# Expansion stage of a three-layer graph network: 0/1 matrices of four groups in one comparison, block numbers four to a word

## The chip, the cores and the metric

The kernel runs on one core of a Trainium2 chip. The metric is the device time of one execution in microseconds (us). A core has engines that run at the same time and meet at semaphores: PE (TensorE: matmuls, with its weight loads shown as PEld), DVE (VectorE), ACT (ScalarE), POOL (GpSimd) and SP, which here only issues DMAs. Sixteen DMA engines move data between HBM and the core.

## The reference

`x` is the embedding of 12500 nodes, 128 wide; 400000 edges (`row`, `col`, `vals`) are the same in all three layers.

```
def _spmm(row, col, vals, x):
    msg = vals[:, None] * x[col]
    return jax.ops.segment_sum(msg, row, num_segments=N)

def _layer(x_prev, row, col, vals, W_a, b_a, W_b, b_b):
    h = _spmm(row, col, vals, x_prev)
    z = (h + x_prev) @ W_a.T + b_a + h * x_prev @ W_b.T + b_b
    return jnp.where(z >= 0, z, NEG_SLOPE * z)
x = emb[x_ids]
x1 = _layer(x, ...)      # then x2 and x3 the same way
return jnp.concatenate((x, x1, x2, x3), axis=1)
```

## The kernel before

Ahead of the layers, some 3000 us sort the edges twice, the second time by `col`, and build tables. The nodes are cut into 100 blocks of 125. The edges, sorted by the block of their `col`, lie in 896 groups (GROUPS) of 512 (GE), filled up so that a group has edges of one block only. Each layer then has three stages.

**Expansion** makes `vals * x[col]`. For a group, PE multiplies a 0/1 matrix (125 rows of the block by 512 edges) with the block's 125 by 128 piece of `x`. The piece is fp32, cut into three bf16 parts (`x_high`, `x_mid`, `x_low`), so a group takes CH x 3 = 12 matmuls of 128 columns (L968 to L972), each with its own weight load of 128 edges of the matrix. The group's result is one PSUM bank of eight. ACT (even groups, L745) and DVE (odd groups, L1347) multiply it by `vals` into one of MR = 8 buffers `msg`, and SP stores it to HBM (L644, 256 KB).

The 0/1 matrices come in steps. `slot_cols` in HBM has the column numbers. SP loads those of four groups (BATCH, a batch; 4 KB) into one of four rows `col_src` (L636), POOL spreads the row over 128 partitions into one of two buffers `col_row` (L556), and DVE compares two groups at a time with its partition number into `col_hot`, which has room for OHR = 8 groups (`make_hot`, L1330).

PE's loop has 56 bodies (ABODIES) of 16 groups (AU). At the head of each, 16 registers are loaded from `group_at` (L961), one offset of a block per group. PE waits for the 0/1 matrices every two groups (`col_hot_ready`) and for a free bank every group (`msg_ready`). DVE's order in `expand` (L1338) is: the comparison for groups n+6 and n+7, then the message of group n+1. `make_hot` waits for `expanded`, which PE raises after each group, so that the place in `col_hot` is free. SP's order (L638) is: at groups 0, 4, 8 and 12 of a body, wait until POOL has spread that batch of this body and load the same batch of the next body, then go on storing messages.

**Sums** (L975 to L982, L1366) gather the messages by `row` with indirect DMAs and add them up with matmuls. **Dense** (L983 to L1018) is the layer's arithmetic on 50 pairs of blocks, written out without a loop on PE. A loop over the layers stands around all three (L956 on PE).

Of the kernel before, what the change touches and what calls it, by code (L numbers as in the profile page):

```python
# [20 lines left out]
I32 = mybir.dt.int32  # L21
# [5 lines left out]
P = 128  # L27
# [55 lines left out]
ABODIES = GROUPS // AU  # L83

# [33 lines left out]
def graph_layers(nc, ids, row, col, vals, emb, weights, biases, out):  # L118
    ctx = ExitStack()
    with ctx:  # L120
# [11 lines left out]
        group_offsets = dram("group_offsets", [P, GTW], I32)  # L132
# [38 lines left out]
        start_groups = sb("start_groups", [P, GTW], I32)  # L171
# [88 lines left out]
        group_at = wi[0:1, TBL0 + 2 * TB:TBL0 + 2 * TB + GROUPS]  # L260
# [180 lines left out]
        def _(pool):  # L441
# [107 lines left out]
            with pool.Fori(0, LAYERS) as la:  # L549
                def spread_cols(i, first):  # L550
                    for h in range(CB):
                        pool.wait_ge(col_src_in[h], la * (ABODIES * DMA) + i * DMA + DMA)
                        if not first or h >= CR2:
                            pool.wait_ge(col_hot_ready, la * (GROUPS // 2) + i * (AU // 2) + (h + 1 - CR2) * BATCH // 2)
                        taken_up()
                        g.partition_broadcast(col_row[:, h % CR2, :], col_src[h * 32:h * 32 + 1, :], channels=P).then_inc(col_spread[h], 1)  # L556

                spread_cols(0, True)
                with pool.Fori(1, ABODIES) as i:
                    spread_cols(i, False)  # L560
                for n in range(MR):
                    pool.wait_ge(msg_stored[n], la * (GROUPS // MR * DMA) + GROUPS // MR * DMA)
                pool.wait_ge(slots_stored, DMA)
                taken_up()
                with pool.Fori(0, BBODIES // 2) as i:
                    for h in range(2):
                        pool.wait_ge(idx_ready, la * BBODIES + i * 2 + (h + 1))
                        for n in range(BU):
                            pool.wait_ge(part_ready, la * TB + i * (2 * BU) + (BCREDIT - BU + h * BU + n + 1))
                            taken_up()  # L570
                            pool.indirect_dma_start(  # L571
                                out=ck[:, n, :, :].rearrange("p h x -> p (h x)"), out_offset=None, in_=flat,
                                in_offset=bass.IndirectOffsetOnAxis(ap=idx[:, h * BU + n:h * BU + n + 1], axis=0),
                            ).then_inc(gathered[n], DMA)

        @block.sync
        def _(sp):
# [45 lines left out]
            sp.dma_start(group_offsets, start_groups[:, :]).then_inc(offsets_stored, DMA)  # L623
# [3 lines left out]
            sp.dma_start(group_at, group_offsets.rearrange("p t -> (p t)")[0:GROUPS].rearrange("(a t) -> a t", a=1)).then_inc(offsets_in, DMA)  # L627
# [6 lines left out]
            with sp.Fori(0, LAYERS) as la:  # L634
# [3 lines left out]
                def store_messages(i, last):  # L638
                    for n in range(AU):
                        if n % BATCH == 0 and not last:  # L640
                            sp.wait_ge(col_spread[n // BATCH], la * ABODIES + i + 1)
                            load_cols(i + 1, n // BATCH)
# [5 lines left out]
                with sp.Fori(0, ABODIES - 1) as i:  # L648
                    store_messages(i, False)
                store_messages(ABODIES - 1, True)  # L650
# [143 lines left out]
        def _(pe):  # L794
# [161 lines left out]
            with pe.Fori(0, LAYERS) as la:  # L956
# [3 lines left out]
                with pe.Fori(0, ABODIES) as i:  # L960
                    _, offs = nc.values_load_multi_w_load_instructions(  # L961
                        group_at[0:1, bass.ds(i * AU, AU)], engines=[mybir.EngineType.PE],
                        min_val=0, max_val=(NB - 1) * D, skip_runtime_bounds_check_because="the table holds offsets of blocks")
                    for n in range(AU):
                        if n % 2 == 0:
                            pe.wait_ge(col_hot_ready, la * (GROUPS // 2) + i * (AU // 2) + (n // 2 + 1))
                        pe.wait_ge(msg_ready[n % 2], la * (GROUPS // 2) + i * (AU // 2) + (n // 2 + 1))
# [53 lines left out]
        def _(dve):  # L1021
# [254 lines left out]
            v.tensor_scalar(start_groups[:, :], w[17][:, 0:GTW], float(D), None, ALU.mult).then_inc(offsets_ready, 1)  # L1276
# [31 lines left out]
            with dve.Fori(0, LAYERS) as la:  # L1308
# [21 lines left out]
                def make_hot(i, n):  # L1330
                    if n % BATCH == 0:
                        dve.wait_ge(col_spread[n // BATCH], la * ABODIES + i + 1)
                    dve.wait_ge(expanded, la * GROUPS + i * AU + (n + 2))
                    v.tensor_scalar(col_hot[:, n % OHR * GE:(n % OHR + 2) * GE],  # L1334
                                    col_row[0:BLK, n // BATCH % CR2, n % BATCH * GE:(n % BATCH + 2) * GE],
                                    iota_c[0:BLK, :], None, ALU.is_equal).then_inc(col_hot_ready, 1)

                def expand(i, first, last_body):  # L1338
                    for n in range(0, AU, 2):
                        m = n + OHR - 2  # L1340
                        if m < AU:
                            make_hot(i, m)
                        elif not last_body:
# [8 lines left out]
                for n in range(0, OHR - 2, 2):  # L1352
# [75 lines left out]
```

## Time and profile before

| | |
|---|---|
| median of 3 runs | 8945.59 us (8935.71 to 8948.48) |
| the profiled execution | 8948.78 us |
| its span | 8947.1 us |
| expansion, three layers | 765.5, 762.1 and 762.8 us |
| busy share of the span | PE 89%, PEld 82%, DVE 79%, POOL 63%, ACT 51% |

Engines named in the rows: PEld is the weight load of a matmul; PEldq, DVEq, SPq are the parts of an engine that read instructions, do register arithmetic and hand work on (the sequencers). A bracket behind a row is the idle time of the engine before it and what ended it. "issue" is time in which the engine waited for nothing that the profile shows. DMA queues of kind "instruction" carry the programs of the engines themselves.

### The profile page before, as it was taken

The numbers are of one execution on the slowest core, as the hardware profiler recorded it, in microseconds if no ns is written. First come the engines' busy times: TensorE is split into PE (matmuls) and PEld (weight loads), VectorE is DVE, ScalarE is ACT, GpSimd is POOL, SyncE is SP. The second block draws the span as 40 slices with busy tenths as digits, with TensorE's granted clock in tenths as the row PEclk, the third lists the DMA queues.
The fourth block names the chain that finished last, engine by engine and source line by source line (L and its number), as shares of the span: only waits on it lengthen the run. The fifth ranks groups of instructions, "written<-read, shape, count | busy, mean of one in ns | idle before, by whom it ended". The sixth has DMA issues, their size and how long they took to land.

```text
span 8947.1 us, 257893 instructions
## 1 busy us (share of the span) xinstructions
PE 7924.2 (89%) x84296; PEld 7333.9 (82%) x84297; DVE 7107.3 (79%) x10046; ACT 4558.1 (51%) x14210; POOL 5595.2 (63%) x3638
## 2 busy tenths in 40 slices
PE   5999986799995688899999788899999788899999
PEld 4777775577773588799999788799999788899999
DVE  8999988799996877777777777777777777777777
ACT  0999990799993366611112566511112566511112
POOL 4788774588783233388886233488885333488884
PEclk8999995899996799999999999999999999999999
DMA  2111111211119988888886588888886688888885
GB/s 78 7 7 7 7 7 38 34 7 7 7 7 30 155 309 312 302 282 287 286 286 247 209 309 307 301 284 286 286 286 224 235 307 310 297 284 287 287 286 200
DMA packets 1005688, 1721.41 MB, mean 192 GB/s; under 512 B 378356, under 2 KB 429624, under 8 KB 1004920
## 3 DMA queue, kind: packets, MB, share of 16 engines
q0 software_dynamic: 378656, 958.17, 35.5%
q1 hardware_dynamic: 499680, 753.27, 23.7%
q10 hardware_dynamic: 127224, 8.24, 3.6%
q8 instruction: 84, 1.38, 0.1%
q14 instruction: 44, 0.36, 0.0%
HBM read 963.06 MB, written 756.12 MB: 192 GB/s over the span
## 4 chain that ended last, share of the span: by engine, by line
PE 56%; DVE 5%; issue 3%; DMA 3%; ACT 1%; DVEq 1%; SPq 0%; POOL 0%; POOLq 0%; ACTq 0%
PE ps L980 37%; PE ps L971 17%; DMA messages<-work 2%; DVE work L1334 2%; DVE hT L1297 1%; PE ps L1008 1%; PE ps L988 1%; PE ps L1009 1%; DVE work L1347 1%; ACT work L745 1%; SPq L644 0%; DVEq L1355 0%; PE ps L998 0%; DVE work L1321 0%; DVE hT L1359 0%
## 5 line engine op out<-in xcount | busy, mean ns | idle before, releaser
L980 PE MATMUL ps<-work 128*128 128x125 f32 x28416 | 3281.9, 278 | 45.8 <-DVE work L1363 45.5
L980 PEld LDWEIGHTS ps<-work 128*128 128x128 f32 x28416 | 3240.4, 192 | 87.2 <-DVE work L1363 46.9
L571 POOL DMA_INDIRECT work<-messages,work x1776 | 2708.8, 1525 | 615.9 <-issue 608.4
L971 PE MATMUL ps<-xb,work 125*128 x10752 | 1909.2, 222 | 450.8 <-DVE work L1334 426.3
L1363 DVE TENSOR_TENSOR work<-work,iota_p 128x1000 f32<-128x1000 f32 x1776 | 2120.0, 1194 | 0.4
L556 POOL PARTITION_BROADCAST work<-work x672 | 890.8, 1326 | 1854.9 <-DMA work<-slot_cols 903.6
L745 ACT ACTIVATE work<-ps,work 128x128 f32<-128x128 f32 x5376 | 1537.1, 369 | 960.4 <-PE ps L971 918.0
L971 PE MATMUL ps<-hT,work 125*128 x10752 | 1904.4, 221 | 0.0
L971 PE MATMUL ps<-work 125*128 x10752 | 1898.5, 220 | 0.0
L763 ACT ACTIVATE work<-work 128x8 f32<-128x8 f32 x1776 | 534.4, 301 | 2675.5 <-DMA work<-messages,work 2675.5
L870 PEld LDWEIGHTS ps<-hT 128*128 128x128 f32 x12768 | 1484.0, 196 | 297.1 <-ACT stage L668 227.3
L870 PE MATMUL ps<-hT 128*128 128x96 f32 x12768 | 1520.1, 280 | 186.6 <-ACT stage L668 186.3
L522 POOL DMA_INDIRECT sorted_edges<-stage,run_idx x798 | 1452.3, 1820 | 307.9 <-issue 237.5
L679 ACT ACTIVATE hT<-iota_p,place 128x128 f32<-128x128 f32 x5320 | 1580.2, 389 | 125.9 <-DVE place L1161 82.8
L971 PEld LDWEIGHTS ps<-xb,work 125*128 125x128 bf16 x10752 | 1047.0, 97 | 479.5 <-issue 479.5
L1347 DVE TENSOR_TENSOR work<-ps,work 128x512 f32<-128x512 f32 x1344 | 920.9, 685 | 636.0 <-PE ps L971 614.4
L1374 DVE TENSOR_TENSOR hT<-hT,ps 128x125 f32 x1776 | 505.8, 285 | 808.1 <-PE ps L980 808.1
L971 PEld LDWEIGHTS ps<-work 125*128 125x128 bf16 x10752 | 1046.6, 97 | 9.5
L971 PEld LDWEIGHTS ps<-hT,work 125*128 125x128 bf16 x10752 | 1052.4, 98 | 1.9
L1334 DVE TENSOR_SCALAR work<-work,iota_c 125x1024 bf16<-125x1024 bf16 x1344 | 885.8, 660 | 0.0
L1154 DVE TENSOR_REDUCE place<-ps 128x24 f32<-128x2400 f32 x266 | 706.5, 2656 | 110.1 <-ACT hT L682 96.6
L512 POOL TENSOR_TENSOR hT<-hT,work 128x672 f32<-128x672 f32 x266 | 363.2, 1366 | 428.6 <-DVE hT L1174 428.6
(212 smaller groups left out, 5680.8 us busy)
## 6 DMA issues: line engine op xcount, KB each, us to landing
messages<-work SPq DMA_DIRECT2D x2688, 256.0 KB, 3.2
work<-messages,work POOLq DMA_INDIRECT x1776, 5.9
out_x<-xb SPq DMA_DIRECT2D x150, 125.0 KB
sorted_edges<-stage,run_idx POOLq DMA_INDIRECT x798
work<-slot_cols SPq DMA_DIRECT2D x672, 4.0 KB
work<-lane_places SPq DMA_DIRECT2D x532, 5.2 KB, 2.1
out_x<-xb ACTq DMA_DIRECT2D x4, 1562.5 KB
sorted_edges<-hT SPq DMA_DIRECT2D x4, 908.0 KB
```

What stands on the lines that cost most here:

```text
L522: pool.indirect_dma_start(out=sorted_edges[p], out_offset=bass.IndirectOffsetOnAxis(ap=run_idx[:, q, k:k + 1], axis=0), in_=stage[:, q, k ...
L556: g.partition_broadcast(col_row[:, h % CR2, :], col_src[h * 32:h * 32 + 1, :], channels=P).then_inc(col_spread[h], 1)
L571: pool.indirect_dma_start(out=ck[:, n, :, :].rearrange("p h x -> p (h x)"), out_offset=None, in_=flat, in_offset=bass.IndirectOffsetOnAxis ...
L679: last = s.activation(to_part[q][:, k, :], iota_p[:, :], ACT.Abs, bias=place[:, q, 2, k:k + 1], scale=-1.0)
L745: last = s.activation(msg[:, n % MR, j * D:(j + 1) * D], ps[:, n % PR, j * D:(j + 1) * D], ACT.Copy, scale=val_now[:, n * CH + j:n * CH + ...
L870: last = t.matmul(ps[:, 6 + q, 0:2 * SLOTS], to_part[q][:, k, :], moved[q][:, k, :, :].rearrange("p f c -> p (f c)"), start=k == 0, stop=k ...
L971: last = t.matmul(ps[:, n % PR, j * D:(j + 1) * D], col_hot[:, at:at + P], piece[:, bass.ds(offs[n], D)], start=k == 0, stop=k == 2)
L980: last = t.matmul(part[n], ck[:, n, j // CH, j % CH * D:(j % CH + 1) * D], sel[:, n % SELB, j, :], start=j == 0, stop=j == CHB - 1)
L1154: v.tensor_reduce(at, ps[:, 0:BANKS, 0:BANKW].rearrange("p k (b l) -> p l k b", l=LANES), AX.XY, ALU.max).then_inc(rank_read, 1)
L1334: v.tensor_scalar(col_hot[:, n % OHR * GE:(n % OHR + 2) * GE], col_row[0:BLK, n // BATCH % CR2, n % BATCH * GE:(n % BATCH + 2) * GE], iota ...
L1347: v.tensor_tensor(msg[:, (n + 1) % MR, :].rearrange("p (j d) -> p j d", j=CH), ps[:, (n + 1) % PR, :].rearrange("p (j d) -> p j d", j=CH), ...
L1363: v.tensor_tensor(sel[:, n % SELB, :, :], row_rel[:, n, :][:, :, None].to_broadcast([P, CHB, BLK]), iota_p[:, 0:BLK][:, None, :].to_broadc ...
```

## The change

It touches the expansion only, and the table that feeds it.

- DVE: one comparison makes the matrices of four groups (125x2048) where two made them; it stands ahead of the messages of groups n+1 and n+3 and makes groups n+4 to n+7. PE waits for `col_hot_ready` once in four groups.
- SP: the load of a batch is issued 24 groups ahead of its use in SP's order where it was 16.
- The table of blocks holds numbers of one byte, so that one 32-bit word has four. PE's loop has 14 bodies of 64 groups, each with one load of 16 registers. The offset of a group is worked out by a shift, a mask and a product.

```
-                with pe.Fori(0, ABODIES) as i:
-                    _, offs = nc.values_load_multi_w_load_instructions(
-                        group_at[0:1, bass.ds(i * AU, AU)], engines=[mybir.EngineType.PE],
-                    for n in range(AU):
-                        if n % 2 == 0:
-                            pe.wait_ge(col_hot_ready, la * (GROUPS // 2) + i * (AU // 2) + (n // 2 + 1))
+                with pe.Fori(0, ABODIES // LB) as i:
+                    _, four = nc.values_load_multi_w_load_instructions(
+                        group_at[0:1, bass.ds(i * (LB * AU // 4), LB * AU // 4)], engines=[mybir.EngineType.PE],
+                    for n in range(LB * AU):
+                        offset = ((four[n // 4] >> (n % 4 * 8)) & 255) * D
+                        offset.max_val = (NB - 1) * D
+                        if n % BATCH == 0:
+                            pe.wait_ge(col_hot_ready, la * (GROUPS // BATCH) + i * (LB * AU // BATCH) + (n // BATCH + 1))
...
-                                                piece[:, bass.ds(offs[n], D)], start=k == 0, stop=k == 2)
+                                                piece[:, bass.ds(offset, D)], start=k == 0, stop=k == 2)
...
-                    dve.wait_ge(expanded, la * GROUPS + i * AU + (n + 2))
-                    v.tensor_scalar(col_hot[:, n % OHR * GE:(n % OHR + 2) * GE],
-                                    col_row[0:BLK, n // BATCH % CR2, n % BATCH * GE:(n % BATCH + 2) * GE],
+                    dve.wait_ge(expanded, la * GROUPS + i * AU + (n + BATCH))
+                    v.tensor_scalar(col_hot[:, n % OHR * GE:(n % OHR + BATCH) * GE],
+                                    col_row[0:BLK, n // BATCH % CR2, :],
...
-                        m = n + OHR - 2
-                        if m < AU:
+                        m = n + OHR - BATCH
+                        if n % BATCH == 0 and m < AU:
...
+                        if n % BATCH == 0 and h < CR2 and left >= 1:
+                            sp.wait_ge(col_spread[CR2 + h], la * ABODIES + i + 1)
+                            load_cols(i + 1, CR2 + h)
+                        if n % BATCH == 0 and h >= CR2 and left >= 2:
+                            sp.wait_ge(col_spread[h - CR2], la * ABODIES + i + 2)
+                            load_cols(i + 2, h - CR2)
```

Two places show what the compiled programs make of it. On PE, the head of the loop's body and its second group, before and then after. L961 and L972 are the loads of the registers; ISA and REGISTER_ALU are the sequencer's own work, waits and register arithmetic; a MATMUL stands for a weight load and a matmul.

```order
L961 TENSOR_LOAD work
L966 ISA
L971 ISA [waits msg_ready0,col_hot_ready]
L971 MATMUL ps<-xb,work 128x128
L971 REGISTER_ALU
...
L971 ISA [waits msg_ready1]
L971 MATMUL ps<-xb,work 128x128
```

```order
L972 TENSOR_LOAD work
L980 ISA
L981 ISA [waits col_hot_ready]
L985 REGISTER_ALU [waits msg_ready0]
L985 ISA
L985 MATMUL ps<-xb,work 128x128
L985 REGISTER_ALU
...
L985 REGISTER_ALU [waits msg_ready1]
L985 REGISTER_ALU
L985 ISA
L985 MATMUL ps<-xb,work 128x128
```

One to two REGISTER_ALU now stand between a group's wait and its first matmul. Counted over the whole body, with a weight load and a matmul as two instructions, it has 444 instructions before (58 of them ISA and REGISTER_ALU, for 16 groups) and 1892 after (354 of them, for 64 groups).

On DVE, the start of the expansion from the last comparison ahead of the first message on, before and then after. TENSOR_SCALAR is a comparison, TENSOR_TENSOR a message, REGISTER_ALU the sequencer's arithmetic.

```order
L1334 TENSOR_SCALAR work<-work,iota_c 125x1024 [waits expanded]
L1345 REGISTER_ALU
L1347 TENSOR_TENSOR work<-ps,work 128x512 [waits expanded]
L1334 TENSOR_SCALAR work<-work,iota_c 125x1024 [waits expanded,col_spread2]
L1345 REGISTER_ALU
L1347 TENSOR_TENSOR work<-ps,work 128x512 [waits expanded]
L1334 TENSOR_SCALAR work<-work,iota_c 125x1024 [waits expanded]
L1345 REGISTER_ALU
L1347 TENSOR_TENSOR work<-ps,work 128x512 [waits expanded]
```

```order
L1347 TENSOR_SCALAR work<-work,iota_c 125x2048 [waits expanded]
L1358 REGISTER_ALU
L1360 TENSOR_TENSOR work<-ps,work 128x512 [waits expanded]
L1358 REGISTER_ALU
L1360 TENSOR_TENSOR work<-ps,work 128x512 [waits expanded]
L1347 TENSOR_SCALAR work<-work,iota_c 125x2048 [waits expanded,col_spread2]
L1358 REGISTER_ALU
L1360 TENSOR_TENSOR work<-ps,work 128x512 [waits expanded]
L1358 REGISTER_ALU
L1360 TENSOR_TENSOR work<-ps,work 128x512 [waits expanded]
```

Before, every message of DVE has a comparison of two groups ahead of it; after, every second one has a comparison of four.

## Rows read from the trace of the kernel before

**Rows 1.** The page: busy time of each engine, and the chain by line.
```profile
PE 7924.2 (89%) x84296; PEld 7333.9 (82%) x84297; DVE 7107.3 (79%) x10046; ACT 4558.1 (51%) x14210; POOL 5595.2 (63%) x3638
...
PE ps L980 37%; PE ps L971 17%; DMA messages<-work 2%; DVE work L1334 2%; DVE hT L1297 1%; PE ps L1008 1%; PE ps L988 1%; PE ps L1009 1%; DVE work L1347 1%; ACT work L745 1%; SPq L644 0%; DVEq L1355 0%; PE ps L998 0%; DVE work L1321 0%; DVE hT L1359 0%
```

**Rows 2.** Busy time by stretch: three expansions; columns as in the first line.
```profile
core 0: us, PE busy (x) PEld busy (x) DVE busy (x) ACT busy (x) POOL busy (x), PEclk, DMA share, GB/s
3016.00:3781.50 765.50, 651.06 (x10752) 637.57 (x10752) 550.05 (x893) 525.99 (x1846) 290.20 (x222) 0.97 0.84 307
5005.50:5767.60 762.10, 646.95 (x10752) 633.57 (x10752) 552.13 (x892) 525.95 (x1846) 290.45 (x222) 0.98 0.84 308
6992.00:7754.80 762.80, 647.60 (x10752) 634.42 (x10752) 552.24 (x893) 526.03 (x1846) 289.82 (x222) 0.97 0.84 308
```

**Rows 3.** Waits of the first expansion: who waited for whom, us, times, longest.
```profile
PEld ps L971 <- issue: 123.8, 55, 3.1
PE ps L971 <- DVE work L1334: 102.1, 50, 2.5
```

**Rows 4.** One change of body: PEld, DVE, register loads (ns min/median/max, first and last).
```profile
3453.18 0.10 PEld L971 LDWEIGHTS ps<-work 125*128 125x128 bf16 x1
3455.43 0.10 PEld L971 LDWEIGHTS ps<-xb,work 125*128 125x128 bf16 x1 [2.16 <-issue]
...
3452.84 0.48 DVE L1334 TENSOR_SCALAR work<-work,iota_c 125x1024 bf16<-125x1024 bf16 x1
...
L961 PEldq TENSOR_LOAD <-work x55: 1768/2324/3118, 3029.2 to 3767.1; - x55
...
L961 PEldq TENSOR_LOAD <-work x1: 1107/1107/1107, 5003.9 to 5003.9; - x1
```

**Rows 5.** Busy time by stretch: two neighbouring bodies, the layer's first body.
```profile
3455.40:3468.90 13.50, 11.27 (x193) 11.04 (x193) 10.28 (x16) 9.40 (x33) 5.27 (x5) 1.00 0.89 326
3468.90:3483.70 14.80, 12.77 (x193) 12.56 (x193) 9.95 (x16) 9.41 (x33) 5.12 (x4) 0.88 0.74 274
3016.00:3030.00 14.00, 13.87 (x192) 13.56 (x192) 8.81 (x15) 8.68 (x31) 5.39 (x5) 0.79 0.58 213
```

**Rows 6.** Busy time in the middle of a body; DMA issues, KB each, us to landing.
```profile
3447.50:3453.50 6.00, 5.95 (x105) 5.77 (x102) 5.30 (x9) 5.10 (x19) 2.30 (x3) 1.00 0.98 357
...
messages<-work SPq DMA_DIRECT2D x896, 256.0 KB, 3.2
```

**Rows 7.** Instruction queues (packets, MB) in 20:190, 3020:3760, 4978:6960, 4965:4975; PE's work in 20:190.
```profile
q8 instruction: 21, 0.34, 0.9%
...
20.00:190.00 170.00, 106.56 (x2719) 92.84 (x2719) 155.84 (x209) 3.82 (x7) 95.22 (x52) 0.89 0.20 63
...
q8 instruction: 1, 0.02, 0.0%
...
q8 instruction: 9, 0.15, 0.0%
...
q8 instruction: 2, 0.03, 1.3%
q14 instruction: 4, 0.03, 0.9%
```

**Rows 8.** Timeline where the loop over the layers goes back to its start.
```profile
4971.95 0.15 DVE L1309 COPY b_now<-bias 128x1 f32 x1 [3.06 <-issue]
...
4973.22 0.26 ACT L739 ACTIVATE work<-work 128x64 f32<-128x64 f32 x1 [3.28 <-issue]
```

**Rows 9.** Register work of PE's sequencer, 3455.2 to 3456.2: ns, first and last start.
```profile
L971 PEldq ALU_OP  x2: 32/34/36, 3455.5 to 3455.9; - x2
```

**Rows 10.** The comparison (ns min/median/max); costliest groups of the first expansion: messages, broadcasts.
```profile
L1334 DVE TENSOR_SCALAR work<-work,iota_c x1344: 469/477/1615, 3013.8 to 7749.9; 125x1024 bf16<-125x1024 bf16 x192
...
L1347 DVE TENSOR_TENSOR work<-ps,work 128x512 f32<-128x512 f32 x448 | 307.0, 685 | 215.4 <-PE ps L971 209.3
...
L556 POOL PARTITION_BROADCAST work<-work x222 | 291.4, 1312 | 614.4 <-DVE work L1334 371.9 <-DMA work<-slot_cols 242.5
```

More of the change, by code:

```diff
@@ L83 @@
 ABODIES = GROUPS // AU
+LB = 4
 CHB = 8
@@ L636, in load_cols, with store_messages @@
                     sp.dma_start(col_src[h * 32:h * 32 + 1, :], cols_of[bass.ds(i * CB + h, 1), :]).then_inc(col_src_in[h], DMA)
-                def store_messages(i, last):
+                def store_messages(i, left):
                     for n in range(AU):
-                        if n % BATCH == 0 and not last:
-                            sp.wait_ge(col_spread[n // BATCH], la * ABODIES + i + 1)
-                            load_cols(i + 1, n // BATCH)
+                        h = n // BATCH
+                        if n % BATCH == 0 and h < CR2 and left >= 1:
[4 more added lines that the diff above has]
+                            load_cols(i + 2, h - CR2)
                         sp.wait_ge(msg_ready[n % 2], la * (GROUPS // 2) + i * (AU // 2) + (ACREDIT + n // 2 + 1))
@@ L647, in _ @@
                     load_cols(0, h)
-                with sp.Fori(0, ABODIES - 1) as i:
-                    store_messages(i, False)
-                store_messages(ABODIES - 1, True)
+                for h in range(CR2):
+                    sp.wait_ge(col_spread[h], la * ABODIES + 1)
+                    load_cols(1, h)
+                with sp.Fori(0, ABODIES - 2) as i:
+                    store_messages(i, 2)
+                store_messages(ABODIES - 2, 1)
+                store_messages(ABODIES - 1, 0)
                 with sp.Fori(0, DSTEPS // DU) as i:
@@ L959, in _ @@
                 pe.sem_inc(pe_layers, 1)
-                with pe.Fori(0, ABODIES) as i:
-                    _, offs = nc.values_load_multi_w_load_instructions(
-                        group_at[0:1, bass.ds(i * AU, AU)], engines=[mybir.EngineType.PE],
-                        min_val=0, max_val=(NB - 1) * D, skip_runtime_bounds_check_because="the table holds offsets of blocks")
-                    for n in range(AU):
-                        if n % 2 == 0:
-                            pe.wait_ge(col_hot_ready, la * (GROUPS // 2) + i * (AU // 2) + (n // 2 + 1))
-                        pe.wait_ge(msg_ready[n % 2], la * (GROUPS // 2) + i * (AU // 2) + (n // 2 + 1))
+                with pe.Fori(0, ABODIES // LB) as i:
+                    _, four = nc.values_load_multi_w_load_instructions(
+                        group_at[0:1, bass.ds(i * (LB * AU // 4), LB * AU // 4)], engines=[mybir.EngineType.PE],
+                        min_val=0, max_val=(NB - 1) * 0x01010101,
+                        skip_runtime_bounds_check_because="the table holds four numbers of blocks in each word")
+                    for n in range(LB * AU):
[3 more added lines that the diff above has]
+                            pe.wait_ge(col_hot_ready, la * (GROUPS // BATCH) + i * (LB * AU // BATCH) + (n // BATCH + 1))
+                        pe.wait_ge(msg_ready[n % 2], la * (GROUPS // 2) + i * (LB * AU // 2) + (n // 2 + 1))
                         for j in range(CH):
@@ L1339, in expand @@
                     for n in range(0, AU, 2):
-                        m = n + OHR - 2
-                        if m < AU:
+                        m = n + OHR - BATCH
+                        if n % BATCH == 0 and m < AU:
                             make_hot(i, m)
-                        elif not last_body:
+                        elif n % BATCH == 0 and not last_body:
                             make_hot(i + 1, m - AU)
@@ L1350, in expand @@
                                         ALU.mult).then_inc(msg_ready[1], 1)
-                for n in range(0, OHR - 2, 2):
+                for n in range(0, OHR - BATCH, BATCH):
                     make_hot(0, n)
```

19 lines of the change are left out of this document (10 added, 9 removed).

## The prediction

> **What bounds the kernel now.** I read the busy times and the chain on the page first, to see which engine carries the span. PE is busy for 89%, and the two lines of matmuls in loops, the sums (L980) and the expansion (L971), hold 37% and 17% of the chain [rows 1]. The change touches only the expansion, so I then cut out the three expansions: 765.5, 762.1 and 762.8 us, 2290.4 together, in which PE is busy for 651 of 765 [rows 2]. With 56 bodies of 16 groups a body takes 13.6 us. No other engine is near its limit there: DVE 550, ACT 526, POOL 290. The DMA share is 0.84.
>
> The waits tell where PE's rest is. PEld stands idle 123.8 us in 55 waits put down to "issue", one at each change of body after the first, 2.25 us each; the same gaps, seen from the matmuls, are put down to DVE's comparison L1334 [rows 3]. These two can't both be right, and one change of body decides. The last weight load is at 3453.18 and the next at 3455.43. The comparison 3452.84 and those ahead of it had long made the matrices that PE wants, since DVE works six groups ahead. The register load takes 2.32 us in the median of 55 [rows 4]. So the gap is the load of 16 registers, not the 0/1 matrices. It took 1.11 us where the DMA queues were quiet, at the second layer's start.
>
> A gap costs a second time now and then. A usual body lasts 13.5 us at clock 1.00, its neighbour 14.8 at a mean of 0.88: after the gap PE ran at 1.2 instead of 2.4 GHz for a while, for 1.3 us more. Fourteen of 55 bodies show this. The layer's first body, after a long idle stretch, lasts 14.0 at 0.79 without a gap in it [rows 5]. Against 13.5 - 2.3 = 11.2 us without gap that is 2.8 more.
>
> What is next behind PE: in the middle of a body the DMA engines are 0.98 busy at 357 GB/s, so about 364 GB/s is what they give to these stores [rows 6]. A body stores 16 x 256 KB and loads 16 KB, 4.21 MB, or 11.6 us, and PE without a gap takes 11.2. The DMA engines live from PE's gaps.
>
> **The change part by part**, for the 64 groups of one new body (four old ones, 54.5 us now).
>
> *Matmuls.* Unchanged in number: 4 x 11.15 = 44.6 us.
>
> *Register loads.* One where there were four. Three gaps go. With nothing in their place this gives 3 x 2.25 = 6.8 us per new body, and about one more of the slow clock (14 of 55 gaps x 1.3 x 3 = 1.0).
>
> *Register arithmetic.* Before, 58 such instructions per 16 groups, 3.6 a group; after, 354 per 64, 5.5. An ALU_OP takes 34 ns by its record, and right after a gap, where the sequencer isn't held up, the same one of the next group comes 0.4 us later [rows 9]. In that time it does about 3 such steps and hands over 24 instructions, so a step costs 0.13 us at most. Two more a group are 0.07 to 0.26 us, and a group then 0.5 to 0.7 us of the sequencer, beside 0.70 us of matmuls. It stays about level with PE, so this costs 0 to 0.4 us per new body, and its small lead at the end of the body is gone. I take 0.1.
>
> *Size of the loop.* This is the term that decides. The program of an engine comes through DMA queues of its own. In 20:190, where PE runs unrolled code, 21 packets of 16 KB arrive while PE takes 2719 weight loads and 2719 matmuls, 259 instructions per packet [rows 7]. So a body of 444 instructions is under two packets, and one of 1892 is 7.4. During the first expansion from 3020 to 3760 one such packet arrives in all: the loop of 444 stays in the engine. But from 4978 to 6960, one round of the loop over the layers, nine arrive. That loop's code (444, a loop for the sums, and the dense part with fp32 matmuls in two passes) is about 2000 instructions, hardly longer than the new body, and it is fetched anew each round. I expect the same of the new body: eight or nine packets per round, and at the branch back a wait until the first is there.
>
> The price of such a wait is not in the trace for PE, which waits for other work at that place. DVE and ACT show it: 3.06 and 3.28 us of "issue" [rows 8]. In the 10 us around it (160 us of 16 DMA engines) their four packets take 0.9%, 0.36 us each, and PE's two 1.3%, 1.04 us each [rows 7], 0.7 us more. The queues are also fuller. I take 4.1 us, between 3.7 (the quiet price plus 0.7) and 4.9. The register load then comes when the stores have drained, nearer to 1.11 than to 2.32, which takes 0.6 us off the gap: 1.65 in place of 2.25 (1.2 to 2.3).
>
> The Trainium skill speaks to this from both sides. "Runtime: NRT & Kernel Launch", Instruction fetch mechanics, gives PE a store of 2048 instructions, refilled in blocks of 256, and says that a taken branch to a block outside the window of two blocks stalls for a fetch. By the first figure the new body would fit; by the window it would not. The nine packets per round agree with the window.
>
> *Clock.* After 5.8 us of idle I expect PE at 1.2 GHz every time: 1.3 to 2.8 us [rows 5], taken as 2.0.
>
> *Comparison.* One of 2048 columns for two of 1024 at 0.48 us: between 0.48 and 0.96 us, 0.75 taken, 0.2 saved per batch. It lies beside the matmuls, DVE having 28% free. What shrinks is the cover: 4 groups x 0.70 = 2.8 us instead of 6 groups, 4.2. Ahead of the comparison stands one message of 0.69 [rows 10]; 0.69 + 0.75 + 0.1 for semaphores leaves 1.2 us. Behind it on DVE are the messages of n+1 and n+3, for which PE's banks and SP's stores wait; four banks of slack cover 0.3 us of delay. At a layer's start PE waits for a longer first comparison, 0.3 us x 3. Nil.
>
> *Loads of columns.* POOL waits 242.5 us for them now [rows 10]; they come eight groups earlier and that wait turns into one for DVE. SP's new waits are for broadcasts that are done eight groups before. POOL is off the path. Nil, as is the table of bytes, which is loaded once.
>
> *The packets' own load.* Nine of 16 KB beside 17 MB of stores is nothing if they spread over 16 engines. The trace doesn't say whether they do; 0 to 3.4 us (below), 0.8 taken.
>
> Sum: 44.6 + 0.1 + 1.65 + 4.1 + 2.0 + 0.8 = 53.25 us for 64 groups against 54.5. Fourteen per layer, three layers: 42 x 53.25 = 2236 against 2290, 54 us less. On the profiled execution's 8948.8 (span 8947.1 and 1.7 around it) that is 8895; the median of the runs lies 3 us lower, so **8892**. With its terms at their ends: 44.6 + 0 + 1.2 + 3.7 + 1.3 + 0 = 50.8 gives 8790; 44.6 + 0.4 + 2.3 + 4.9 + 2.8 + 0.8 = 55.8 gives 9000.
>
> **The rivals.**
>
> *The new body stays in the engine.* For it: a body of 7.4 packets is a little shorter than the layers' loop. Against it: only a little, and a fetch ahead past its end would push out its start. Then 44.6 + 2.3 + 0.3 for the clock + 0.1 = 47.3 us, with the DMA engines at 4 x 11.6 = 46.4 close below; 1 us for their friction gives 48.3. 42 x 48.3 = 2029, 262 less: 8684; without friction 8642. The Trainium skill's 2048 instructions (same page and section) would give this.
>
> *The fetches slow the stores.* If PE's packets all go through one of the 16 DMA engines, as a queue that only one engine serves would, that one has its 46.4 us of stores and nine packets at 1.04 us, 9.4: 55.8 us. A store of 256 KB is done when all 16 have finished their part, so this one sets PE's pace through the eight message buffers. It turns the gain into a loss from 54.5 us on, that is from nine packets at 0.9 us. With 1 us of friction 56.8: 42 x 56.8 = 2386, 95 more: 9041. Against it: the packets run in PE's gap too, and a packet's time is not all transfer; at the stores' rate 16 KB is 0.7 us.
>
> *The comparison comes late.* The cover of 2.8 us is gone if DVE is held by a full message buffer (msg_stored) ahead of the comparison, or by POOL: the longest comparison was 1.6 us [rows 10]. At 0.3 us for each of 16 batches it adds 4.8 us: 58.0, or 9095. Nothing in the trace of before shows PE waiting inside a body.
>
> *The change does less than it says:* register loads on 16 words could take longer apart from the first; no sign of it.
>
> **How the numbers follow.** Forecast (gap of one fetch, 8790 to 9000) 0.46; stays in the engine (8640 to 8690) 0.18; slowed stores (9000 to 9060) 0.24; late comparisons, or waits at every packet's end as well (9060 to 9200) 0.12. A measurement of this kernel can tell 0.2%, 18 us, from no change. Of the forecast's 0.46 I give 0.34 to faster, 0.07 to the same, 0.05 to slower; of the slowed stores 0.03 to the same. So faster 0.52, same 0.10, slower 0.38. The range leaves out the late comparisons' upper part and the lower half of the body that stays: 8650 to 9075.
>
> **What the profile after would show.** q8 packets: about 42 x 9 = 380 more than now if the body is fetched each round, none if it stays. PEld's "issue" at the head of a body: 42 gaps of 5 to 6.5 us (forecast) or 2.3 us (stays), and none inside. Register loads 42, well under 2.3 us in the forecast. Mean clock in the expansion 0.96 to 0.98. If gaps appear every 8 or 9 groups, fetches are late at each packet. If messages wait for DMA and the landing time of 3.2 us [rows 6] grows past 4, the stores are slowed. I am wrong altogether if PE waits for L1347 inside a batch, or if the time outside the expansion moves.

## The result and the profile after

The changed kernel takes 9065.23 us (median of 4 runs, 9053.16 to 9079.0) against 8947.03 us before (4 runs, 8935.71 to 8954.79), a ratio of 1.0135 (95% interval 1.012 to 1.015). It is slower; the prediction said faster, 8892 us. The profiled execution has a span of 9066.2 us, 119.1 more than before. All but 3 us of it lies in the expansion.

Page after, against [rows 1]: busy time, the instruction queue, the start of the chain by line, the stores:

```profile
PE 8012.8 (88%) x84296; PEld 7379.3 (81%) x84297; DVE 6807.3 (75%) x9374; ACT 4543.7 (50%) x14210; POOL 5572.5 (61%) x3638
...
q8 instruction: 453, 7.42, 0.4%
...
PE ps L994 36%; SPq L651 7%; PE ps L985 6%; DMA messages<-work 5%; SPq L639 1%; DVE hT L1311 1%; PE ps L1022 1%; PE ps L1002 1%; ACT work L756 1%; PE ps L1023 1%; DVE work L1347 1%; DVE work L1360 0%; PE ps L1012 0%; DVE hT L1372 0%; DVE work L1335 0%
...
messages<-work SPq DMA_DIRECT2D x2688, 256.0 KB, 4.0
```

Matmuls in the expansion (now L985) held 17% of the chain and hold 6%. What took their place is SP's issue of the stores (L651, 7% where L644 had 0%) and the stores (5% for 2%). The page of before has 84 packets in q8; 369 more make 42 x 8.8, so the new body is fetched anew in each of its 42 rounds.

The three expansions, cut out as in [rows 2] and with its columns:

```profile
3014.80:3817.50 802.70, 676.23 (x10750) 648.67 (x10751) 452.29 (x669) 520.59 (x1843) 286.84 (x222) 0.94 0.81 294
5043.10:5845.80 802.70, 675.69 (x10751) 648.20 (x10752) 452.15 (x669) 519.99 (x1843) 287.04 (x222) 0.94 0.81 294
7072.60:7873.30 800.70, 680.91 (x10751) 653.17 (x10752) 452.04 (x669) 520.26 (x1842) 287.07 (x222) 0.94 0.81 295
```

37, 41 and 38 us longer, 116 together. DVE has 100 us less to do per layer, and the DMA engines are less busy than before (0.81, 294 GB/s). So no engine is nearer its limit; there is more waiting.

**Where a layer's time goes.** For layer two of each kernel I took the 10751 steps from one weight load of the expansion to the next. Steps at the head of a loop's body are counted whole. Of all others 0.0569 us are the step at full clock, 611 us together (608.6 with 55 heads), and what is above falls to steps of 0.10 to 0.13 us (half clock) or to the rest, here called "inside" the bodies. In us:

| kernel | from first to last | heads | half clock | inside |
|---|---|---|---|---|
| before | 761.8 | 129.8 (55 of 2.36) | 15.8 | 8 |
| after | 802.7 | 83.6 (13 of 6.43) | 29.8 | 78 |

The heads gave back 46 us, the clock took 14, and 70 came up inside the bodies, where before there was almost nothing. The branch back of the loop in PE's sequencer (ns min/median/max) after, the register load behind it, and one head on PEld; then the branch of before:

```profile
L971 PEldq COMPARE_BRANCH  x42: 76/4108/4482, 3064.9 to 7872.9; - x42
...
L972 PEldq TENSOR_LOAD <-work x42: 1118/1920/2360, 3012.9 to 7820.5; - x42
...
3302.68 0.10 PEld L985 LDWEIGHTS ps<-xb,work 125*128 125x128 bf16 x1 [6.75 <-issue]
```

```profile
L960 PEldq COMPARE_BRANCH  x168: 76/213/227, 3028.8 to 7753.7; - x168
```

The branch takes 4.1 us where it took 0.21, exactly as forecast. The register load behind it has a median of 1.92.

**What happens inside a body.** A place far from a head. The chain of 3340 to 3352 by line and three pieces of it (start, us); the DMA engines' busy tenths from 3345 to 3347.5 and the queues' packets there (packets, MB, share of 16 engines); DVE and PEld:

```profile
by line: SPq L651 61.2%; issue 20.1%; SPq L639 10.3%; DVE work L1360 5.6%; SPq L650 2.4%; SPq L658 1.0%; DVEq L1360 0.5%
...
3344.51 0.33 SPq L651
...
3345.04 2.25 SPq L651
...
3348.47 0.34 SPq L651
...
DMA  7998997799879987998684121111103002000100
...
q1 hardware_dynamic: 289, 0.51, 56.6%
q8 instruction: 1, 0.02, 4.6%
...
3346.33 0.74 DVE L1347 TENSOR_SCALAR work<-work,iota_c 125x2048 bf16<-125x2048 bf16 x1
3348.81 0.69 DVE L1360 TENSOR_TENSOR work<-ps,work 128x512 f32<-128x512 f32 x1 [1.74 <-DMA messages<-work]
...
3350.60 0.74 DVE L1347 TENSOR_SCALAR work<-work,iota_c 125x2048 bf16<-125x2048 bf16 x1
...
3351.69 0.10 PEld L985 LDWEIGHTS ps<-xb,work 125*128 125x128 bf16 x1 [1.33 <-issue]
```

It reads as a chain of four steps. A packet of PE's program arrives: its record starts at 3345.08 and lasts 1.84 us. SP's issue of a store, 0.33 us otherwise, starts at 3345.04 and takes 2.25; meanwhile the DMA engines run dry (the right half of their row). DVE's next message then waits 1.74 us for its buffer to be stored. The comparison stands behind that message and one more, starts at 3350.60, ends at 3351.34, and PE, which had used up its four groups of matrices, loads weights again at 3351.69 after 1.33 us. SP doesn't wait for anything in this stretch: where no load of columns stands between them, its issues of stores follow each other every 0.52 to 0.59 us. The experiments ask which links are needed.

### The profile page after: what moved, and what is told of

It reads as the page before. It is cut to its first block, busy times and chain, and to the rows that moved or that the text cites. A ratio compares the mean times of both kernels' runs of the same rounds, so it can differ in the third digit from the quotient of the medians.

```text
span 9066.2 us, 260455 instructions
## 1 busy us (share of the span) xinstructions
PE 8012.8 (88%) x84296; PEld 7379.3 (81%) x84297; DVE 6807.3 (75%) x9374; ACT 4543.7 (50%) x14210; POOL 5572.5 (61%) x3638
## 4 chain that ended last, share of the span: by engine, by line
PE 45%; SPq 9%; issue 6%; DMA 6%; DVE 4%; ACT 1%; DVEq 0%; POOL 0%; ACTq 0%; POOLq 0%
PE ps L994 36%; SPq L651 7%; PE ps L985 6%; DMA messages<-work 5%; SPq L639 1%; DVE hT L1311 1%; PE ps L1022 1%; PE ps L1002 1%; ACT work L756 1%; PE ps L1023 1%; DVE work L1347 1%; DVE work L1360 0%; PE ps L1012 0%; DVE hT L1372 0%; DVE work L1335 0%
## 5 line engine op out<-in xcount | busy, mean ns | idle before, releaser
L985 PE MATMUL ps<-xb,work 125*128 x10752 | 1966.0, 225 | 479.6 <-issue 245.5
L985 PE MATMUL ps<-hT,work 125*128 x10752 | 1959.7, 223 | 0.4
L985 PE MATMUL ps<-work 125*128 x10752 | 1948.7, 223 | 0.6
L985 PEld LDWEIGHTS ps<-xb,work 125*128 125x128 bf16 x10752 | 1060.0, 99 | 524.3 <-issue 521.6
L985 PEld LDWEIGHTS ps<-work 125*128 125x128 bf16 x10752 | 1057.8, 98 | 36.2 <-issue 2.5
L985 PEld LDWEIGHTS ps<-hT,work 125*128 125x128 bf16 x10752 | 1066.3, 99 | 3.2 <-issue 0.5
L515 POOL TENSOR_TENSOR hT<-hT,work 128x672 f32<-128x672 f32 x266 | 389.4, 1464 | 392.7 <-DVE hT L1188 392.5
L693 ACT ACTIVATE hT<-hT 128x2560 f32<-128x2560 f32 x266 | 621.8, 2338 | 8.4
```

## Experiments

All times are medians of 4 to 10 executions beside the kernel before on the same chip (8943 to 8946 us), except three kernels that ran once, which are named. The edits are against the changed kernel where nothing else is said.

The recorded expectations speak of stalls of 58 and 13 us a layer: these count only PE's waits of over 0.3 us inside the bodies. The column "inside" of the tables takes in the short ones too and gives 78 and 48 us for the same two kernels.

**Bodies of 16 and 32 groups.** The fetch is taken away and everything else kept: L84 has LB = 1, and LB = 2.

```
-LB = 4
+LB = 1
```

> The changed kernel with bodies of 16 groups again (476 instructions, a load of 4 registers). Theory of the fetched program: the body is under two packets of 16 KB and stays in the engine, so hardly any q8 packet comes in the expansions and the gap of 6.4 us every 64 groups is gone; a gap of about 1 us per 16 groups stays for the load of 4 registers; body 11.15 + 1.0 = 12.1 us, 56 bodies 680 us a layer against 803, time about 8700. Theory of late comparisons (4 groups of cover): the 3.9 us of stalls inside 64 groups stay, 1.0 per body, 13.1 us, time about 8865. Theory of saturated stores (DMA engines or SP at 11.6 us per 16 groups whatever PE does): no faster than 11.6 plus friction, 12.1 to 12.5, 8700 to 8770.

> The changed kernel with bodies of 32 groups (948 instructions, 3.7 packets, 8 registers). If the engine keeps two packets: fetched in each of 28 rounds a layer, about 140 q8 packets per layer, gap 5.5 to 6.5 us and 2 to 2.5 us of slow clock per 32 groups, 22.3 + 6 + 2.3 + 1 = 31.6 us, 885 us a layer, time about 9310. If it keeps seven or eight: no fetch, gap of about 1.5 us per 32 groups, 24 us, 672 us a layer, time about 8675. Late comparisons alone: between the two, near 8850, with no q8 packets.

Measured: 8805.96 us (ratio 0.9845, 0.9828 to 0.9861) and 8808.28 (0.9844, 0.9828 to 0.9861). No expectation named this time; 8770, the end of the one on the stores, is nearest. One number turns the changed kernel from 1.35% slower into 1.55% faster. The page and the first expansion of LB = 1, its stores, and the register loads (4 words now):

```profile
q8 instruction: 84, 1.38, 0.1%
...
3009.90:3723.90 714.00, 653.75 (x10751) 624.18 (x10752) 452.37 (x668) 522.36 (x1841) 287.71 (x222) 1.00 0.89 328
...
messages<-work SPq DMA_DIRECT2D x2688, 256.0 KB, 4.9
...
L972 PEldq TENSOR_LOAD <-work x168: 329/602/932, 3008.8 to 7593.0; - x168
```

No fetch, the clock at 1.00, and the rest of the change is a gain: a load of 4 words for 16 groups takes 0.60 us where 16 words took 2.32 [rows 4]. That the bodies of 16 and 32 come out alike, though one has 55 heads (63.0 us) and the other 27 (43.8 us) in a layer, says that something else sets the pace of both. The chain names it:

```profile
3207.01 0.85 ACT work L756 x3
...
3208.02 4.81 DMA messages<-work
...
3214.23 5.00 DMA messages<-work
...
3220.63 5.26 DMA messages<-work
```

A message buffer is written, stored in 4.8 to 5.3 us, and written again every 6.2 to 6.4 us. Eight buffers make 0.80 us a group, 12.8 us for 16, 715 us a layer.

**Comparison of two, six groups ahead, in the fetched body.** DVE's order of before (with POOL's and PE's counts of `col_hot_ready` for it) under the new loop of 64 groups.

```
-                    dve.wait_ge(expanded, la * GROUPS + i * AU + (n + BATCH))
-                    v.tensor_scalar(col_hot[:, n % OHR * GE:(n % OHR + BATCH) * GE],
-                                    col_row[0:BLK, n // BATCH % CR2, :],
+                    dve.wait_ge(expanded, la * GROUPS + i * AU + (n + 2))
+                    v.tensor_scalar(col_hot[:, n % OHR * GE:(n % OHR + 2) * GE],
+                                    col_row[0:BLK, n // BATCH % CR2, n % BATCH * GE:(n % BATCH + 2) * GE],
...
-                        m = n + OHR - BATCH
-                        if n % BATCH == 0 and m < AU:
+                        m = n + OHR - 2
+                        if m < AU:
```

> The changed kernel with the comparisons of before (two groups at a time, six ahead), bodies of 64 groups kept. Theory of late comparisons: the 3.9 us of stalls inside 64 groups go, 42 x 3.9 = 164 us less, about 8900. Theory of the fetched program and the stores: nothing changes beyond 0.5%, about 9065, head gaps of 6.4 us and stalls inside stay.

Measured: 8981.65 us (1.0041, 1.0027 to 1.0055), halfway between the two expectations. The same 453 packets and the same heads (13 of 6.41 us), but 48 us inside a layer's bodies in place of 78. So the comparison is worth 84 us of the 118, though the prediction had it at nil.

**The comparison of four alone**, with the table and the bodies of before and SP's earlier loads.

```
-                with pe.Fori(0, ABODIES // LB) as i:
+                with pe.Fori(0, ABODIES) as i:
...
+                        group_at[0:1, bass.ds(i * AU, AU)], engines=[mybir.EngineType.PE],
...
-                        offset = ((four[n // 4] >> (n % 4 * 8)) & 255) * D
...
-                                                piece[:, bass.ds(offset, D)], start=k == 0, stop=k == 2)
+                                                piece[:, bass.ds(offs[n], D)], start=k == 0, stop=k == 2)
```

> The kernel before with only two parts of the change: comparisons of four groups and SP's earlier loads; table and bodies of 16 groups with 16 registers as before (448 instructions). Theory of late comparisons: 1.0 us more per body, 168 bodies, about 9115. Theory of the fetched program: as before within 0.5%, 8947, PE's gaps of 2.25 us unchanged.

Measured: 8951.74 us (1.0005, 0.9995 to 1.0015): no difference. The longer comparison and the shorter cover cost nothing as long as nothing is late. So "nil" is right here and wrong in the fetched body: the two parts of the change cost more together than the sum of each.

**Which of the two, size or distance?** Comparisons of two groups as above, but four groups ahead as in the changed kernel. The edit is against the kernel with six ahead.

```
-                        m = n + OHR - 2
+                        m = n + OHR - 4
```

> lb4_hot2 (bodies of 64 groups, comparisons of two groups) with the comparison four groups ahead instead of six: only the cover changes, not the size of the comparison. If the shorter cover is why PE stalls inside the fetched body (58 us a layer in the changed kernel, 13 in lb4_hot2), the stalls come back: 45 to 80 us a layer, time 9065 to 9150. If the size of the comparison or the rarer release of col_hot is why: they stay at about 13 us and the time at 8982.

Measured: 9070.68 us (1.0142, 1.0125 to 1.0159), the changed kernel's time within 0.1%. It is the distance: two groups less of cover cost 89 us, and the comparison's size nothing. The trace agrees: who waited for the comparison between 5070 and 5700 us (us, times), first in the changed kernel, then with six ahead, then with four ahead in twos:

```profile
  POOL work L559: 323.4, 131
  PE ps L985: 90.8, 40
```

```profile
  POOL work L559: 320.8, 136
  PE ps L985: 67.4, 19
```

```profile
  POOL work L559: 337.8, 130
  PE ps L985: 84.4, 39
```

The stretch has eleven heads, whose gaps are put down to the comparison as they were before [rows 3]. With six ahead there are eight waits more, with four ahead 28 and 29.

**Comparisons of two without fetches**, in bodies of 16 and 32 groups.

```
-LB = 4
+LB = 1
...
-                        m = n + OHR - BATCH
+                        m = n + OHR - 2
```

> Only the packed table is kept of the change together with SP's earlier loads: bodies of 16 groups, load of 4 registers, comparisons of two groups six ahead. If the pace of lb1 (715 us a layer) is set by the stores' bytes alone: the same, 8806, within 0.3%. If the shorter cover costs there too (44 us of stalls a layer beside the register loads): those fall to some 15 us and the expansion to about 690, time 8730.

> As lb1_hot2 with bodies of 32 groups and a load of 8 registers. Stores' bytes alone: 8808 as lb2. Shorter cover: about 8730, a little below lb1_hot2 if the rarer register load counts.

Measured: 8811.0 us (0.9853, 0.9836 to 0.9869) and 8809.74 (0.9849, 0.9833 to 0.9866), with four ahead 8806 and 8808. Where nothing is fetched, the distance makes no difference. The same view in the same stretch, LB = 1 with four ahead, then with six:

```profile
  PE ps L985: 7.2, 12
```

```profile
  PE ps L985: 9.5, 13
```

**A body that is just shorter.** Three of four groups take block 0 instead of their own, which leaves out the choice of block (the messages are not the right ones) and its instructions: 1652 in place of 1892, with the same 64 groups and register loads.

```
-                                                piece[:, bass.ds(offset, D)], start=k == 0, stop=k == 2)
+                                                piece[:, bass.ds(offset, D)] if n % 4 == 0 else piece[:, 0:D], start=k == 0, stop=k == 2)
```

> The changed kernel, bodies of 64 groups and the load of 16 registers kept, but three groups of four take a fixed block instead of working out their offset (left out: the choice of the block), so that the body is 1652 instructions instead of 1892: 6.5 packets of 16 KB. If the engine keeps about seven packets, it stays: about 84 q8 packets in all, a gap of about 2.3 us per 64 groups, and the time falls to that of lb1 and lb2, 8806, where the stores set the pace. If it is fetched all the same: about 42 x 8 = 336 q8 packets more than before, head gaps of 6.4 us, time 9000 to 9060.

Measured: 8785.9 us (0.9825, 0.9809 to 0.9841), with this line on its page:

```profile
q8 instruction: 99, 1.62, 0.1%
```

A loop of 1652 instructions (6.4 packets at 259 each) stays in the engine; 1892 (7.3) doesn't, and neither do the 1908 (7.4) that the trace has in a body of the kernel with comparisons of two, whose waits for the matrices are twice as many. The heads fall from 6.43 to 2.13 us, the register load alone, and a layer from 802.7 to 708.0. The missing instructions themselves are a small part of these 95 us at most, since LB = 1 has them in every group and needs 715.

**No loop.** The 14 bodies are written out, so that PE's program is fetched once a layer in a straight line.

```
-                with pe.Fori(0, ABODIES // LB) as i:
+                for i in range(ABODIES // LB):
```

> The changed kernel with PE's 14 bodies of 64 groups written out one behind the other: the same instructions, arithmetic and register loads, about 103 packets a layer fetched in sequence, no branch back. If the wait at the branch (4 us and the slow clock behind it) is what costs: head gaps fall from 6.4 to about 2 us, 42 x (4.4 + 1.5) = 248 us less, 8820. If the packets cost by themselves, because SP's issue of a store is held up by each (about 0.8 us each, one per 8.7 groups), the stalls inside the bodies stay and long issues of SP stay at about 300: with them added to the pace of the stores 820 us a layer, 9050; with them half hidden 8930.

Measured: 8841.46 us (0.9888, 0.9871 to 0.9904), near the first expectation, 8820. Its page and second expansion:

```profile
q8 instruction: 387, 6.34, 0.3%
...
4971.40:5697.50 726.10, 664.52 (x10751) 631.24 (x10752) 451.74 (x669) 520.03 (x1843) 287.42 (x222) 0.99 0.89 325
```

It has 303 packets more than LB = 1, 101 a layer, where the changed kernel has 123 more, and it loses 11 us a layer to LB = 1, not 87. So packets as such need not cost much. A straight line keeps PE fed: its heads are 2.05 us, and the 4.1 us of the branch and its slow clock are gone. The packets come all the same, and 85 of SP's issues in layer two still take over 0.7 us.

**Half of each store.** In layers two and three the messages' stores write half of every row (128 KB for 256; the sums then gather what layer one left there). Layer one is as it was. One execution each, in the changed kernel, in LB = 1, and with comparisons of two, six ahead.

```
-                        sp.dma_start(messages[bass.ds(i * (AU * P) + n * P, P), 0:CH * D], msg[:, n % MR, :]).then_inc(msg_stored[n % MR], DMA)
+                        sp.dma_start(messages[bass.ds(i * (AU * P) + n * P, P), 0:W], msg[:, n % MR, 0:W]).then_inc(msg_stored[n % MR], DMA)
...
+            sp_layer(0, CH * D)
+            with sp.Fori(1, LAYERS) as la:
+                sp_layer(la, CH * D // 2)
```

> The changed kernel, where in the second and third layer SP stores only half of each message (left out: the other half of the columns), so the same number of issues and half the bytes. If stalls inside the 64 groups come from saturated DMA engines: they go, 44.6 + 6.0 + 2.5 = 53 us, 742 us per layer in place of 803, landing time 2.5 us or less. If they come from SP's issue being held up by the fetches: the long issues stay, as many as packets, but with fewer bytes in flight they cost PE less. The head gaps are the fetch's either way and stay at 5.5 to 6.4 us, about 60 clear gaps being due to nothing else.

> lb1 (bodies of 16 groups, load of 4 registers) with half of each message stored in layers two and three (left out: the other half of the columns). If the stores' bytes set lb1's pace (720 us a layer, 12.9 per body): a body falls to 11.15 + 0.9 = 12.0 us, 675 us a layer. If SP's issues set it (0.68 us per group uncontended) or the late comparisons: it stays above 700.

> lb4_hot2 with half of each message stored in layers two and three (left out: the other half of the columns). Stalls inside the body fall from 13 us to about nothing, the 13 head gaps stay at 5.5 to 6 us each: layers two and three of the expansion 735 to 750 us against 771. The long issues of SP stay at one per program packet, about 115 a layer. If instead PE itself waits for late packets inside the body, gaps without any wait of DVE or ACT remain.

Measured: 9014.16, 8686.02 and 8969.11 us. Second expansion of the first two:

```profile
5044.60:5817.50 772.90, 665.76 (x10751) 648.38 (x10752) 454.79 (x669) 512.23 (x1845) 287.05 (x222) 0.94 0.47 155
```

```profile
4947.40:5606.40 659.00, 632.71 (x10751) 619.18 (x10752) 455.95 (x669) 524.11 (x1845) 287.83 (x222) 1.00 0.54 179
```

Without fetches, half the bytes free PE: 659 us for 715, and 7 us inside the bodies. That confirms the stores as the floor of LB = 1. In the fetched body the DMA engines are 0.47 busy and 55 us are still lost inside the bodies of a layer (51 with six ahead, where 735 to 750 us a layer were expected and 766.6 came). 111 of SP's issues in layer two take over 0.7 us, each next to one of the 124 packets. So a fetch delays the stores by itself, not by taking bandwidth that is short. Full stores make layer two 30 us longer with four groups ahead (772.9 to 802.7) and 5 with six ahead (766.6 to 771.2); in layer three it is 25 and 9. So the short cover costs most where fetches and full stores meet; with half stores it costs 6 us in layer two and 11 in layer three.

**The table again**, layer two of all kernels that were read this way:

| kernel | first to last | heads | half clock | inside | packets on the page |
|---|---|---|---|---|---|
| LB = 1 | 715.2 | 63.0 (55 of 1.15) | 3.7 | 40 | 84 |
| LB = 2 | 715.5 | 43.8 (27 of 1.62) | 3.1 | 58 | 90 |
| 1652 instructions | 708.0 | 27.7 (13 of 2.13) | 5.8 | 63 | 99 |
| no loop | 726.1 | 26.6 (13 of 2.05) | 14.2 | 74 | 387 |
| twos, six ahead | 771.2 | 83.3 (13 of 6.41) | 28.7 | 48 | 453 |
| twos, four ahead | 804.8 | 84.9 (13 of 6.53) | 34.3 | 75 | 453 |
| LB = 1, half stores | 659.0 | 41.0 (55 of 0.74) | 2.5 | 7 | 84 |
| changed, half stores | 772.9 | 74.6 (13 of 5.74) | 32.1 | 55 | 453 |

In the first three, heads, clock and inside add up to nearly the same (107, 105, 97), however many heads there are: PE waits for the stores, at a head or elsewhere. So their "inside" is no loss of its own.

**SP has no time to spare.** The waits of SP tie these results together. SP issues all the stores and the loads of columns. Its waits for a message in layer two, from the first weight load to the last (us, times, longest), in LB = 1, without the loop, in the changed kernel, and with twos six ahead:

```profile
SPq L651 <- ACT work L756: 56.6, 136, 1.3
SPq L651 <- DVE work L1360: 15.0, 45, 0.8
```

```profile
SPq L651 <- ACT work L756: 9.7, 18, 1.4
SPq L651 <- DVE work L1360: 4.7, 11, 0.9
```

```profile
SPq L651 <- ACT work L756: 65.8, 42, 4.5
SPq L651 <- DVE work L1360: 10.0, 20, 1.3
```

```profile
SPq L651 <- ACT work L756: 28.6, 41, 1.8
SPq L651 <- DVE work L1361: 10.5, 22, 1.3
```

In LB = 1 SP waits 72 us of 715; the other 644 are its own work, 11.5 us per 16 groups, where PE needs 11.2. So SP can't make up for a long issue while PE runs. In straight code the 85 long issues take 68 us more than issues of 0.33 would. They fill the time in which SP would have waited for messages, 14 us of waiting are left, and the layer is only 11 us longer: there SP sets the pace. In the changed kernel 99 long issues take 86 us more, and SP waits 76 us all the same, about two thirds of it around the 13 heads, where PE is at its branch and hands nothing on. Both losses add up, and a layer is 802.7 = 641 + 86 + 76. With six groups ahead the long issues cost no less (96 us), but SP waits 39 us. That PE, with two groups more of cover, comes to the head with more groups waiting to be stored would explain this; it is argued, not shown.

## Why the prediction was wrong, point by point

Per 64 groups the changed kernel takes 802.7 / 14 = 57.3 us, the sum said 53.25. 9065 lies inside the stated 8650 to 9075, but by luck: the range was drawn around the rivals, and the forecast's own terms ended at 9000. They ended there because the high sum took 0.8 for the packets, though the text gives up to 3.4; with 3.4 it would have been 9108.

- **Matmuls, register arithmetic**: right within 1 us. 611 us for 14 bodies are 43.7; the 44.6 and 0.1 of the sum held small waits besides. The arithmetic isn't seen: LB = 1 has it and runs at the stores' pace.
- **Size of the loop**: right: 8.8 packets a round where eight or nine were expected, one gap at each head, the branch 4.1 us where 3.7 to 4.9 were given. (1892 instructions at 259 a packet are 7.3 packets, not 7.4, and the trace has 452 in a body of before where 444 were counted; neither matters here.) The register load did not fall to 1.11; with 1.92 a head is 6.43 us, and 13 heads for 14 bodies make 5.97 where 5.75 was taken.
- **Clock**: right. 29.8 us over 14 bodies are 2.1 us, 2.0 was taken. ("Fourteen of 55" bodies of before with a slow stretch are 12, 10 and 11 in the three layers.) The mean clock came out at 0.94, below the 0.96 to 0.98 that I named.
- **"The packets' own load", 0.8 us: the first step that failed.** It counted the packets as bytes on the DMA engines. Those are small indeed, 4.6% of 16 engines in the window above. But a packet holds up the store that SP is issuing. Between 3100 and 3700 us 93 packets arrive, and 75 of SP's issues take over 0.7 us, each of them within 2 us of a packet and in the median 0.28 us after its start; in LB = 1, without packets, none does. The stores' issues of this stretch in both kernels (ns min/median/max):

```profile
L651 SPq DMA_DIRECT2D messages<-work x664: 332/333/2256, 3099.9 to 3699.6; - x166
```

```profile
L651 SPq DMA_DIRECT2D messages<-work x749: 332/332/685, 3101.1 to 3699.5; - x188
```

  In place of 0.8 us stand 48 us a layer even with a cover of six groups, 3.4 per 64, and only 8 us a layer of them were there before. The prediction has no term for SP's own time, which left nothing to absorb these delays.
- **"Comparison ... Nil": the second step that failed.** Its 0.75 us was exact (740 to 776 ns), and its cover of 2.8 us against 1.4 of work was right too. But the cover was held against the delays that the trace of before shows. It had to be held against those that the fetches make: the 1.2 us that were left are less than the 1.74 that DVE's message waited above. That is 78 - 48 = 30 us a layer, 2.1 per 64 groups, 84 to 89 us in all. The two failed terms are 78 / 14 = 5.6 us where 0.8 stood, and the sum with all terms as measured is 43.7 + 6.0 + 2.1 + 5.6 = 57.4. These are shares of one measured layer, so they must add up; what each is worth rests on the experiments.
- **The rivals.** "The comparison comes late", with waits at the packets (9060 to 9200, 0.12) named the half that decided, and its 9095 is nearest to 9065. But it looked for the delay in DVE's buffer or in POOL without its cause, the fetch. "The fetches slow the stores" (9041) had the other half. Both were weighed as alternatives, and each was held against a program in which the other did not happen. (9095 leaves out the 3 us that the other sums take off for the median; with them it is 9091.)
- **"The new body stays in the engine" was priced too low**: 8684, where LB = 1 gives 8806. The stores' limit of 11.6 us for 16 groups was worked out from 357 GB/s in 6 us [rows 6]. Sustained, with eight buffers in turn, 328 GB/s are reached, landing goes from 3.2 to 4.9 us, and 16 groups take 12.8. Loops that stay in the engine got 140 us from this change (LB = 1) or 157 (1652 instructions, the choice of block left out), not 262.
- **Loads of columns**: right. POOL's wait for them vanishes (903.6 to 192.7 us in the kernel with comparisons of four alone) and gives nothing.

As for the Trainium skill, "Runtime: NRT & Kernel Launch", Instruction fetch mechanics: it gives PE a store of 2048 instructions and a window of two blocks of 256 for branches. The runs agree with neither as a limit for a loop: 1652 instructions are more than two blocks and branch back without a fetch, and 1892 are fewer than 2048 and are fetched.

**What stays open.** The limit lies between 1652 and 1892 instructions; nothing between was run. What it is in SP's issue that a packet holds up, no run here shows. The straight code with 101 packets more a layer loses 11 us, the fetched loop with 123 more and a branch loses 87, of which heads and clock are 47 (83.6 + 29.8 against 63.0 + 3.7). SP's waits above account for the rest, but no run took work off SP to test that, and no run gave LB = 1 more message buffers to see whether the stores' pace would rise.

## What to carry to other kernels

Unrolling a loop to save its head pays only while its program stays in the engine: count the body's instructions on the busiest engine, look whether the instruction queue's packets grow with the rounds of a loop of that length, and prefer the shortest body whose head costs nothing in the end. Here bodies of 16 groups with packed numbers are as fast as any kernel that computes everything, 8806 us, 1.6% under the kernel before and 2.9% under the changed one. Weigh two edits of one change together: a cover is to be held against the delays that the other edit brings, not against those in the trace of before. And look at the engine that only issues DMAs: SP, with 11.5 us of work per 16 groups beside PE's 11.2, had nothing left to catch up with.

## What the runs showed of the hardware that was not expected

- Packets of PE's program (16 KB each) lengthen SP's issue of a store from 0.33 to between 0.76 and 2.26 us: 75 such issues with 93 packets in 600 us, and the DMA engines run dry meanwhile.
- A loop on PE of up to 1652 instructions is not fetched again; one of 1892 or more is, 8.8 packets each round, and the branch back takes 4.1 us in place of 0.21 under this load.
- Stores of 256 KB from eight buffers in turn run at 0.98 share and 357 GB/s over 6 us, but hold 0.89 and 328 GB/s over 700 us.
- The load of registers costs by their number: 16 take 2.3 us while stores run (1.1 without), 8 take 1.12 and 4 take 0.60.
